# The opening of a two-layer graph network kernel, written out row by row: folded weights spread over three rows, spare TensorE products added, function table and index tiles loaded ahead

## The reference

```python
h = jnp.maximum(_layernorm(x, axis=-1), 0.0)
# layer 0
h_nodes = _mlp2(h, node_W1, node_b1, node_W2, node_b2)      # 128 -> 64 -> 64, silu between
h_edges = _mlp2(edge_attr, edge_W1, edge_b1, edge_W2, edge_b2)
msg_in = jnp.concatenate([h_nodes[dst], h_nodes[src], h_edges], axis=-1)
msgs = _mlp2(msg_in, msg_W1, msg_b1, msg_W2, msg_b2)
agg = segment_sum(msgs, dst) / jnp.maximum(counts, 1.0)[:, None]
upd = _mlp2(jnp.concatenate([h, agg], axis=-1), upd_W1, upd_b1, upd_W2, upd_b2)
x = x + layernorm(h + upd) * ln_g + ln_b
# layer 1
h = jnp.maximum(_layernorm(x, axis=-1), 0.0)
# h @ W, attention over each node's in-edges and itself, sum of h[src] * alpha
x = x + attention(h, edge_index, W, att_src, att_dst) + bias
```

## Time and profile before

| | |
|---|---|
| time, median of 3 runs | 4091.2 us (4089.45 to 4092.23) |
| profiled execution, time | 4091.22 us |
| profiled execution, span | 4089.1 us |
| TensorE busy | 3382.9 us (83%) |
| VectorE busy | 2517.0 us (62%) |
| ScalarE busy | 2850.5 us (70%) |
| GpSimd busy | 2965.8 us (73%) |
| first instruction of the message pass | 109.75 us |
| first gather of the attention pass | 2109.75 us |

### The profile page before, as it was taken

The page is one execution under the profiler, slowest core; times in us unless marked ns, Lnnn a source line. Parts: engine busy times, 40 slices in busy tenths (PEclk is TensorE's granted clock), DMA queues, the critical chain, the costliest instruction groups (busy, mean ns, idle before and its releaser), DMA issues. The chain is left out here.

```text
span 4089.1 us, 126775 instructions
## 1 busy us (share of the span) xinstructions
PE 3382.9 (83%) x30848; PEld 2976.2 (73%) x30849; DVE 2517.0 (62%) x10511; ACT 2850.5 (70%) x5940; POOL 2965.8 (73%) x3134
## 2 busy tenths in 40 slices
PE   7789888999988899999947777777777778777777
PEld 4677777777777788888847777777777767766776
DVE  5752222222222256777748777777777777888888
ACT  6466565656556577788738777777777777877777
POOL 2677777777777777777737777777777777777774
PEclk8789999999899899999967777777777777777777
DMA  5322222222222233333342222222222222332332
GB/s 159 88 60 53 54 55 53 56 53 53 55 54 53 60 83 91 91 96 95 81 120 58 57 58 58 57 58 58 58 57 58 58 58 63 79 78 76 78 78 58
DMA packets 319769, 282.90 MB, mean 69 GB/s; under 512 B 143418, under 2 KB 242924, under 8 KB 319532
## 3 DMA queue, kind: packets, MB, share of 16 engines
q0 software_dynamic: 99456, 159.33, 15.9%
q1 hardware_dynamic: 139224, 79.62, 7.4%
q10 hardware_dynamic: 80852, 41.75, 3.5%
HBM read 249.58 MB, written 29.40 MB: 68 GB/s over the span
## 5 line engine op out<-in xcount | busy, mean ns | idle before, releaser
L541 POOL DMA_INDIRECT a_G<-Htab,idx x1554 | 1470.8, 946 | 526.3 <-issue 464.0
L541 POOL DMA_INDIRECT p_rows<-Btab,idx x1554 | 1471.4, 947 | 475.1 <-issue 473.4
L1799 PE MATMUL a_psA<-a_GP,a_S 128*128 128x132 f32 x4704 | 892.5, 365 | 2.7 <-DVE a_GP L1634 2.7
L1799 PEld LDWEIGHTS a_psA<-a_GP,a_S 128*128 128x128 f32 x4704 | 821.5, 268 | 8.2 <-DVE a_GP L1634 3.1
L1056 DVE TENSOR_TENSOR p_z<-p_psZ,p_rows 128x512 f32<-128x512 f32 x294 | 195.9, 689 | 829.4 <-SPq L746 679.6
L1206 ACT COPY p_ST<-p_psT 128x1024 bf16<-128x1024 bf16 x294 | 300.5, 1022 | 563.7 <-PE p_psT L1318 543.4
L1730 ACT CAST a_S<-a_Sb 128x512 f32<-128x512 bf16 x588 | 608.6, 1144 | 0.0
L1365 PE MATMUL p_psA<-p_msg,p_S 128*128 128x65 f32 x4704 | 589.9, 284 | 10.9 <-ACT p_S L1227 9.8
L1365 PEld LDWEIGHTS p_psA<-p_msg,p_S 128*128 128x128 f32 x4704 | 571.6, 201 | 16.5 <-issue 12.8
L1227 ACT CAST p_S<-p_Sb 128x1024 f32 (+1 forms) x294 | 582.6, 1982 | 0.0
L1341 PEld LDWEIGHTS p_psZ<-wc,p_s 128*128 128x128 f32 x2352 | 325.1, 206 | 204.7 <-issue 103.5
(11 more groups left out here) (212 smaller groups left out, 5165.8 us busy)
## 6 DMA issues: line engine op xcount, KB each, us to landing
arena<-in_ea SPq DMA_DIRECT2D x196, 256.0 KB
p_single<-Btab SPq DMA_DIRECT2D x1792, 0.2 KB
a_single<-Htab SPq DMA_DIRECT2D x1792, 0.5 KB
p_rows<-Btab,idx POOLq DMA_INDIRECT x1554
a_G<-Htab,idx POOLq DMA_INDIRECT x1554
Htab<-u_H ACTq DMA_DIRECT2D x49, 136.0 KB
arena<-Htab SPq DMA_DIRECT2D x7, 952.0 KB
n_x<-in_x SPq DMA_DIRECT2D x14, 448.0 KB, 4.0
```

The lines of the kernel that those rows point to most:

```text
L541: pool.indirect_dma_start(out=rows[:, u * C + c, :], out_offset=None, in_=table, in_offset=bass.IndirectOffsetOnAxis(ap=idx[u][:, c:c + 1] ...
L1799: m = pe.matmul(psA[v][:, 0:HR], S32[v][:, c, :], GP[v][:, c, :], start=c == 0, stop=c == C - 1)
```

## The change

1. `open_rows` takes the place of `run_pairs` in the opening: all nine rows are written out, no loop; GpSimd's 14 powers too.
2. VectorE's fold is cut in three: `fold` (`wab`, `cA`, `wc2`) after row 0, `fold_heads` (`m2` and the heads' weights) after row 1, `fold_rest` (`iota_nc`, `identb`) after row 2. TensorE's fold stays whole after row 0.
3. After each pass from row 1 on TensorE makes BUSY = 3 products of `ident` by itself, 128 x 128 in float32, into `pscX`, which nobody reads. The first waits until `wc2` is copied out of `pscX`.
4. ScalarE issues ten of the weight loads and SP sixteen (13 and 13 before): `lnb`, `wcat` and `attd` move to SP. After its third load ScalarE runs one silu on two columns, `n_warm`, that VectorE has zeroed.
5. SP loads the first seven index tiles in the opening, behind the weights, and no longer at the start of the message pass.

```diff
-            for to, src in loads[0::2]:
+            for to, src in loads[0:20:2] + loads[20:]:
                 sp.dma_start(to, src).then_inc(s_w, 16)
             ...
+            for u in range(SLOTS):
+                sp.dma_start(k["idx"][u][:, :], t["src"][u * P:(u + 1) * P, :]).then_inc(k["slots"][0][u], 16)
...
-            with pool.Fori(0, NG) as g:
+            for g in range(NG):
...
                         m.then_inc(s_T, 1)
-            run_pairs(pe, body, NG, 3, first=fold)
+                    if row > 0:
+                        if row == 1 and u == 0:
+                            pe.wait_ge(s_v, NODE_BIAS + 4)
+                        for _ in range(BUSY):
+                            pe.matmul(psX[:, 0:P], k["ident"][:, :], k["ident"][:, :], start=True, stop=True)
+            open_rows(pe, body, [fold])
...
-            for to, src in loads[1::2]:
+            for n, (to, src) in enumerate(loads[1:20:2]):
                 act.dma_start(to, src).then_inc(s_w, 16)
+                if n == 2:
+                    act.wait_ge(s_zero, 1)
+                    act.activation(warm[:, 1:2], warm[:, 0:1], ACT.Silu)
...
-            run_pairs(dve, body, NG, 3, first=fold)
+            open_rows(dve, body, [fold, fold_heads, fold_rest])
...
+def open_rows(eng, body, parts=()):
+
+    def edge(j, back):
+        return 0 <= j - back < NG
+    for row in range((NG + 4) // 2):
+        body(row, edge)
+        if row < len(parts):
+            parts[row]()
...
-    for u in range(SLOTS):
-        load_idx(u, u)
     for u in range(SLOTS - 1):
         load_ea(u, u)
```

More of the change, by code:

```diff
@@ L54 @@
 LINKS = 11
+BUSY = 3
 MAGIC = 0x5F3759DF
@@ L232, in opening @@
     ve, half = sb("n_ve", [P, GW]), sb("n_half", [P, GW])
-    s1 = sb("n_s1", [H, GW * P])
+    s1, warm = sb("n_s1", [H, GW * P]), sb("n_warm", [P, 2])
     psT, psU, psV = (ctx.enter_context(nc.psum_tensor(f"n_ps{n}", [P, 2, 512], F32)) for n in "TUV")
@@ L292, in body @@
                         load(g + 2, u)
-            run_pairs(sp, body, NG, 3)
+            open_rows(sp, body)
             sp.wait_ge(s_wc, 32)
@@ L390, in body @@
                                   k["xs"][:, bass.ds(g * GW, GW)]).then_inc(s_h, 1)
-            run_pairs(act, body, NG, 3)
+            open_rows(act, body)
         @block.vector
@@ L395, in _ @@
             fold_link = Count()
+            dve.memset(warm[:, :], 0.0)
             dve.memset(k["ew1"][:, :], 0.0).then_inc(s_v, 1)
@@ L419, in fold, with fold_heads @@
                 dve.wait_ge(s_v, link())
+                assert link.n == NODE_BIAS + 4
+            def fold_heads():
+                link = fold_link
                 dve.wait_ge(s_pe, 4)
@@ L428, in fold, with fold_rest @@
                     dve.wait_ge(s_v, link())
+            def fold_rest():
+                link = fold_link
                 dve.wait_ge(s_id, 3)
@@ L487, in lay_iota, with run_pairs @@
     return dve.tensor_copy(words(psI[:, :, :]), words(k["iota_nc"][:, :, :]))
-def run_pairs(eng, body, count, depth, first=None):
+def run_pairs(eng, body, count, depth):
     def edge(j, back):
@@ L497, in run_pairs @@
         body(row, edge)
-        if row == 0 and first is not None:
-            first()
     with eng.Fori(3, count // 2 - 1) as row:
```

## The result

| | before | after |
|---|---|---|
| time, median of 13 runs each, side by side | 4090.79 us (4086.47 to 4094.74) | 4083.1 us (4080.34 to 4087.95) |
| ratio | | 0.9981 (95% interval 0.9973 to 0.9988) |
| profiled execution: time, span | 4091.22, 4089.1 | 4080.34, 4078.6 |
| first gather of the message pass | 112.13 | 102.83 |
| first gather of the attention pass | 2109.75 | 2099.31 |

A forecast was written before the change was run, and what follows sets the result against it. GpSimd's gathers were a rigid block, so the gain was the first gather's shift: +2.0 - 1.3 - 3.2 - 0.5 - 1.4 = -4.4 us, from 4091.2 to 4086.8, range 4082.0 to 4092.0.

The forecast's parts named there:

- rival A: Opening's weight loads: the queues do not matter, fold starts at 16.0 to 16.5; -7.9 us, 4083.3; chance 0.17.
- Rival C: Opening: rival A with passes of 5.6 us and a trio for nothing; -9.3 us, 4081.9; chance 0.09.
- Weights to SP: Opening: loads moved to SP's queue delay the fold's start from 16.00 to 19.5, putting n_h(2) +2.0 us.
- The step behind it: Opening, TensorE: n_h(2) comes 8.9 us after the fold's start, through T(1), two copies, shift and hand-overs.
- Third n_x: Opening, SP's queue: load issued near 16 behind the other loads, moments of pass 2 near 22.8; costs 0.4 at most.
- n_h(2) to n_h(4): Early opening passes: n_h(4) comes 11.4 to 11.5 us behind n_h(2), against 12.70 before; -1.3 us.
- Nine passes: Opening, n_h(4) to n_h(13): with trios 5.75 us a pass, 51.75 in place of 54.99; -3.2 us.
- Tail: Opening after n_h(13), to the meeting: one U had run at half clock, two trios come in; -0.5 us.
- start of the gathers: Head of the message pass: first gather at pass start + 1.0, not + 2.4, with index tiles loaded ahead; -1.4 us.
- Table 0: Opening, ScalarE's table load: n_h(0) comes earlier, but T(0) only waits longer for the fold behind it; 0 us.
- Written-out loops: Opening passes: branches and computed counts cost some 0.1 us a hand-over, included in the 5.75 us per pass.
- Both passes: Message and attention passes: nothing gained inside; gathers stay rigid at 1.25 us each and move with the first gather.

The follow-up runs named there:

- e7: Changed kernel with 16-bit-word tables, plus four more one-row-to-128-partition loads on SP's queue ahead of attd; fold's first product +6.8 us, no time given.
- e8: Changed kernel with 16-bit-word tables, plus four more one-row-to-128-partition loads at the end of ScalarE's queue; fold's first product +5.8 us, no time given.
- e4: Kernel before plus the spare products alone, in loop form, table values read as low 16-bit halves; median 4121.17 us.
- e3: Changed kernel without the spare TensorE products, table values read as low 16-bit halves; median 4121.59 us.
- e1: Control: kernel before with table values read as the low 16-bit halves of the 32-bit words, nothing else; median 4128.68 us.
- e5: Control: kernel before with two tables holding 16-bit words, on a second, slower chip; median 6893.0 us, 1.0047 of before.
- e2: Control: changed kernel with table values read as the low 16-bit halves of the 32-bit words, nothing else; median 4120.46 us.
- e11: e9 with only the index-tile loads put back at the head of the message pass; median 4114.63 us.
- e9: Changed kernel with two tables holding 16-bit words, on a third chip; median 4114.47 us, 1.0053 of before.
- e10: e9 with three buffers for the node features in place of two; median 4109.14 us.
- e12: e9 with the fold in one piece behind row 0, the spare products kept; median 4119.59 us.

## Why the prediction was right, and where not

The time, 4083.1, lies in the range (4082.0 to 4092.0) and within 0.2% of before, the outcome that had 0.81. But the sum behind 4086.8 had a wrong first term, and the rival A, to which I gave 0.17, named both the fold's start (16.0 to 16.5, measured 16.24) and the time (4083.3). Rival C's shift of -9.3, to which I gave 0.09, is that of the profiled first gather. The range held because it took in A; by its own sum the forecast was right only in part.

- **Weights to SP, +2.0 on n_h(2): failed.** The step "a queue is thus slow on such loads, and a second queue goes beside it, not instead" fell. SP's queue alone moved 153 packets per us where it had moved 94, and e7 and e8 give 1.7 and 1.5 us per load on either queue. So 94 was not a queue's limit. From 10.5 to 12.5 us the two queues of the earlier trace rows moved 150 per us together, about what SP's reaches alone now; why it fell to 94 afterwards no run shows. The Trainium skill, DMA: Bandwidth & Descriptors, section Issuing engines are not separate DMA queues, says that DMAs of several issuing engines run on the same 16 DMA engines and that issuing from more of them saves only the time of issue; here the fold's start, 16.24 for 16.00, agrees with it. The step behind it held: n_h(2) came 9.01 behind the fold (8.9 forecast), at 25.25: -1.15.
- **Third n_x:** issued at 15.93 (near 16 forecast), its statistics at 20.58 and not 22.8; the fold's weights had landed by 16.24.
- **n_h(2) to n_h(4): right in kind,** -1.76 for -1.3: V of the first passes ran at full clock (1.82 us at 29.68). e4, the products alone, shows the same 11.07 us; e3, without them, had no fall here either and took 10.98.
- **Nine passes: 51.18 for 51.75,** -3.81 for -3.2. In all ten profiles with the products the granted clock stayed at 1.00 from 24 us to TensorE's last product of the opening; in all four without them (before, e1, e3, e5) it fell. What a kernel without them loses differs by execution: 54.99, 51.42, 51.88, 59.53. So -3.8 is one draw. A trio was put at 0.04 us; V follows it without a pause in half the passes and mostly after some 0.5 us of issue in the others, and e2 against e3 gives some 0.1 a pass.
- **Tail -1.12 for -0.5; start of the gathers -1.46 for -1.4.** Before's fourth fall lay in the tail, 15.68 us long; in e1 to e4 and after, none of which has a fall there, it took 14.5 to 14.6. e11 gives 1.13 for the index tiles. The held gather stayed one, -0.3.
- **Table 0: fits.** T(0) began at 11.96 for 13.29, and TensorE then waited 2.56 us for the weights in place of 0.99. Written-out loops have no run of their own.
- **Both passes: 0.** The message pass took 1996.48 for 1997.62 from its first gather to the attention pass's, the rest 1979.29 for 1979.35. The gather block is rigid as said, and in this pair the time followed its start. The repeats do not show this as well: in the profiles of e1 and e2, and of e9 and e10, the lead of 5.3 and 4.3 us was gone at the first gather of the attention pass, though the medians lean the same way (8.2 and 5.3 us, intervals overlapping). The step that the attention pass starts a fixed time behind the gathers thus holds in the mean at best, and on the chip of e5 the medians do not follow at all.

In sum -9.30 at the first gather where -4.4 was forecast: 3.15 from n_h(2) (-1.15 for +2.0: the fold started 3.26 us ahead of the forecast 19.5, and n_h(2) came 0.11 later behind it), and 1.75 from terms of the right kind and too small. Of the -9.30, 6.69 are the three terms in which before had its four falls, in this one profile. The medians show 7.7.

## What to carry to other kernels

A low DMA share in a stretch with slow loads does not say that the queue is the limit (20% before and 41 to 81% after went with much the same loads); before pricing a move between queues, ask whether the same loads would be as slow on the other one, and try it with a few more of them. Spare products in TensorE's gaps, where the next product waits anyway, cost some 0.1 us a pass here and take away a loss that differs from run to run. Once they are in, look again at the buffers: a third `n_x` gives 4 us more of the opening (e10); it was run with the 16-bit tables alone, so that its time in the kernel as it stands, some 4078 us (4083.1 less the 5.3 between the medians of e9 and e10), is an estimate. A gain of a few us ahead of a long pass should be read at more than one later point: here a stretch between the passes scattered by more than the gain.

## What the runs showed that I had not expected

- One chip of three takes 6855 us for the kernel before (4091 to 4096 on the others), with GpSimd's gathers in the message pass 1.10 us apart and not 0.30 (e5), and there 14.6 us saved in the opening are gone at the end. The attention pass gives them back; what bounds it there was not found.
- Reading the tables as 16-bit words costs some 30 us in the attention pass (2009.9 in e9, 1979.3 in after); why is open. Where the tables themselves hold 16-bit words (e5 to e12), one gather early in the message pass is held 4.85 to 5.15 us; in before, after and e1 to e4 it is 2.19 to 2.78.
- The hand-over from the last gather of one pass to the first of the next takes 49.9 to 61.6 us on the two chips of e1 to e4 and e9 to e12 (53.8 before, 52.9 after), a spread above everything that this change could win. It is longer where TensorE has more left to do in it: TensorE is busy for 31.2 of the 49.9 us in e9, 36.1 of 53.8 in before, 39.2 of 56.0 in e12 and 44.9 of 61.6 in e2, with a mean granted clock of 0.64 to 0.76 in all. What sets how far TensorE is behind when the last gather is issued was not found.
